# A selective-scan and mixture-of-experts kernel: the first stretch rebuilt, with the first scan unit fed by TensorE instead of by DMA

## The reference, cut to what matters

```python
xn = x * rsqrt(mean(x * x) + eps) * norm_w          # of the layer-normalised x
xi, z = split(xn @ W_in)                            # 256 channels each
xc = silu(causal_conv(xi, conv_w, 4 taps) + conv_b)
dt, Bm, Cm = split(xc @ W_x, [64, 16, 16])
dt = softplus(dt @ W_dt + b_dt)                     # 256 channels
dA = exp(dt[..., None] * A);  dBu = (dt * xc)[..., None] * Bm[:, :, None, :]
h = scan over time of  h = dA * h + dBu             # 256 channels x 16 states
y = (sum over states of h * Cm + D_skip * xc) * silu(z)
s = xn_in + y @ W_out
# experts: softmax over 8 logits, the two largest kept and renormalised;
# out = sum over experts of score_e * (relu(xn @ W1_e + b1_e) @ W2_e + b2_e)
```

## Time and profile before

| | before |
|---|---|
| median of 3 runs | 320.62 us |
| the profiled execution | 321.84 us |
| its span, first to last instruction | 320.0 us |
| busy: PE, DVE, ACT, POOL | 274.6, 275.3, 223.5, 234.6 us |
| DVE's first product and first scan | start at 38.15 and 39.61 us |
| DVE's last instruction | starts at 316.62 us |

### The profile page before, as it was taken

One profiled execution on the slowest core, in us unless ns is written; L12 is line 12 of the kernel. 1 busy time (PEld: TensorE's weight loads), 2 busy tenths in 40 slices (PEclk: granted clock), 3 DMA queues, 4 the chain that ended last, 5 costly groups with the idle time before them and its releaser, 6 DMA issues. The chain is left out here.

```text
span 320.0 us, 4220 instructions
## 1 busy us (share of the span) xinstructions
PE 274.6 (86%) x1223; PEld 140.9 (44%) x1223; DVE 275.3 (86%) x324; ACT 223.5 (70%) x434; POOL 234.6 (73%) x223
## 2 busy tenths in 40 slices
PE   0682699969899999697999999878999998899983
PEld 0331334434644653134566464126554564462472
DVE  3697299975999989997999989899999999999973
ACT  1157288599858896779758975999675684787620
POOL 2207055458899996666989998849989897889764
PEclk9996959999999999789799999999999999999997
DMA  6929990005182830041743800050289600000002
GB/s 170 306 70 210 246 199 3 0 0 123 39 182 61 197 66 0 0 117 20 161 101 68 199 0 3 0 124 11 59 181 203 152 0 0 2 1 1 0 3 66
DMA packets 16758, 26.76 MB, mean 84 GB/s; under 512 B 4264, under 2 KB 9759, under 8 KB 16735
## 3 DMA queue, kind: packets, MB, share of 16 engines
q1 hardware_dynamic: 16246, 25.44, 34.1%
q10 hardware_dynamic: 488, 1.05, 1.1%
HBM read 8.52 MB, written 1.18 MB: 30 GB/s over the span
## 5 line engine op out<-in xcount | busy, mean ns | idle before, releaser
L376 POOL TENSOR_TENSOR hc<-hs,Ct 128x512 f32<-128x512 f32 x126 | 157.7, 1275 | 34.4 <-DVE hs L807 32.7
L807 DVE TENSOR_TENSOR_SCAN hs<-dec,pdbu 128x1024 f32<-128x1024 f32 x64 | 146.3, 2285 | 8.2 <-ACT dec L507 2.6
L507 ACT ACTIVATE dec<-rep,negA 128x512 f32<-128x512 f32 x128 | 87.6, 722 | 8.7 <-DMA rep<-dt_u 5.7
L798 DVE TENSOR_TENSOR pdbu<-rep,pB 128x1024 f32<-128x1024 f32 x64 | 78.6, 1228 | 11.9 <-DMA rep<-dt_u 6.5
L980 PE MATMUL px<-xnT,w 128*128 128x512 f32 x128 | 65.4, 619 | 7.9 <-ACT xnT L566 5.9
L986 PEld LDWEIGHTS px<-w,hT 128*128 128x128 f32 x512 | 62.0, 196 | 18.7 <-ACT hT L622 9.7
L986 PE MATMUL px<-w,hT 128*128 128x128 f32 x512 | 64.6, 282 | 4.7 <-ACT hT L622 4.7
L622 ACT ACTIVATE hT<-px,cols 128x512 f32<-128x512 f32 x64 | 43.2, 690 | 29.6 <-PE px L980 15.6
L461 POOL TENSOR_TENSOR acc<-acc,ysc 128x512 f32<-128x512 f32 x29 | 37.4, 1290 | 14.1 <-ACT ysc L611 9.5
L611 ACT ACTIVATE ysc<-px,score 128x128 f32<-128x128 f32 x116 | 32.8, 366 | 16.5 <-PE px L986 16.5
L909 PE MATMUL py<-hc,rsel 128*32 128x512 f32 x256 | 41.7, 610 | 1.8 <-POOL hc L376 1.8
(11 more groups left out here) (111 smaller groups left out, 235.9 us busy)
## 6 DMA issues: line engine op xcount, KB each, us to landing
rep<-dt_u SPq DMA_DIRECT2D x124, 128.0 KB, 2.4
Ct<-c_rows SPq DMA_DIRECT2D x16, 256.0 KB, 5.0
w<-in_L_ffn_W SPq DMA_DIRECT2D x1, 1024.0 KB
out<-xn SPq DMA_DIRECT2D x4, 256.0 KB, 2.5
x_sb<-in_L_attn_x SPq DMA_DIRECT2D x1, 768.0 KB, 5.2
hc<-in_L_attn_conv_w ACTq DMA_DIRECT2D x1, 512.0 KB, 4.4
rep<-dt_u ACTq DMA_DIRECT2D x4, 128.0 KB, 3.9
x_sb<-in_L_attn_x SPq DMA_DIRECT2D x1, 256.0 KB, 5.2
```

Source lines behind the costliest of these rows:

```text
L376: eng.tensor_tensor(hc[:, n % HC_RING, i, :], hs[:, n % HS_RING, i, :], Ct[:, k % 2, j, :], ALU.mult).then_inc(hc_last if n == UNITS - 1 e ...
L507: act.activation(dec[:, n % DEC_RING, i, :], rep[:, q, 0, :], ACT.Exp, scale=negA[:, q, j:j + 1])\
L798: dve.tensor_tensor(pdbu[:, :, :], rep[:, 2 * pair:2 * pair + 2, 1, :], pB[:, m % 2:m % 2 + 1, :].to_broadcast([P, 2, CH]), ALU.mult).then ...
L807: dve.tensor_tensor_scan(hs[:, n % HS_RING].rearrange("p b t -> p (b t)"), dec[:, n % DEC_RING].rearrange("p b t -> p (b t)"), pdbu[:, :, ...
```

## The change

x of chunk 0 comes in two halves, issued by SP and by ACT, and each is normalised, transposed and copied on its own. The taps come as one row, which TensorE spreads to `pdbu`; DVE weighs them in eight pieces of 128. Selector matrices are built by POOL instead of DVE. `keep_busy` adds small TensorE matmuls whose result nobody reads. For the first unit TensorE spreads `xc` and the parts of `dt` with selectors `csel` (jobs `x0`, `x1`, `d0`, `d1`): `dec` comes from `d0` and `d1` directly, and `u * B` is built as `dt * (xc * B)`, with `xc * B` formed by POOL. The replicas of the first four blocks are then wanted from unit 1 on, and SP issues blocks 2 and 0, POOL blocks 3 and 1 (ACT none). POOL does the roots of chunks 1 to 3 (`rest_roots`) behind these issues. The C product is one instruction of 1024. The slot numbers of `EARLY`, `TABLE`, `STEPS` and `START` are all new.

```diff
-NORM = [range(0, TPC), range(TPC, TILES)]
+NORM = [range(0, TPC // 2), range(TPC // 2, TPC), range(TPC, TILES)]
-PRE_JOBS = ["tr", "xc0", "xc1", "dt", "v0", "v1", "tn", "m0a"]
+PRE_JOBS = ["tr", "xc0", "xc1", "dt", "x0", "v0", "x1", "v1", "d0", "d1", "tn", "m0a"]
...
-    "silu": [12], "log1p": [13, 16], "correct": [17, 20], "sum_dt": [16, 18], "times_dt": [20, 28],
+    "silu": [11], "log1p": [13, 17], "correct": [18, 20], "sum_dt": [18, 18], "times_dt": [23, 29],
...
-    "gate": [0, 1, 3, 5, 6], "gate_e": [0], "gate_p": [2, 3, 4],
+    "second": [0], "gate": [2, 3, 4, 4, 7], "gate_e": [0], "gate_p": [1, 3, 5],
...
+BUSY = {"row": 8, "rows": 4, "tr": 2, "xc1": 2}
...
+        def replicas(eng, q, soft=False):
+            b, r = divmod(q * GD, P)
+            for i in range(GROUP):
+                eng.dma_start(rep[GD * i:GD * (i + 1), q], dt_u[r:r + GD, b])\
+                    .then_inc(rep_soft[q // 2] if soft else rep_in[q // 2], 16)
...
-            sp.dma_start(x_sb[:, 0], xv_dram[:, 0:TPC, :]).then_inc(x_first, 16)
+            sp.dma_start(x_sb[:, 0, 0:TPC // 2], xv_dram[:, 0:TPC // 2, :]).then_inc(x_in[0], 16)
+            sp.dma_start(win[:, :], W_in[:, :]).then_inc(w_in, 16)
...
                 for q in (2 * pair, 2 * pair + 1):
-                    if k == 0 and q == 1:
-                        continue
...
+                    if k > 0 or q >= 2 * HALF_PAIRS or q % 2 == 0:
+                        replicas(sp, q)
...
-            for i in range(2):
-                eng.tensor_tensor(hc[:, n % HC_RING, i, :], hs[:, n % HS_RING, i, :], Ct[:, k % 2, j, :],
-                                  ALU.mult).then_inc(hc_last if n == UNITS - 1 else hc_done, 1)
+            eng.tensor_tensor(hc[:, n % HC_RING], hs[:, n % HS_RING], Ct[:, k % 2, j:j + 1, :].to_broadcast([P, 2, CH]),
+                              ALU.mult).then_inc(hc_last if n == UNITS - 1 else hc_done, 1)
...
-            inverse_roots(0)
-            inverse_roots(1)
+            first_roots()
+            selectors()
+            pool.wait_ge(B_copied, 1)
+            for i in range(2):
+                wait_emptied(pool, f"x{i}", 0)
+                pool.tensor_tensor(xB[:, i], xB[:, i], B_first, ALU.mult).then_inc(xB_done, 1)
+            pool.wait_ge(far_done, 1)
+            for q in (3, 1):
+                replicas(pool, q, True)
+            rest_roots()
...
-            act.dma_start(cwb.rearrange("p d k -> p (d k)"),
-                          conv_w.rearrange("d a k -> a (d k)").to_broadcast([P, DIN * TAPS])).then_inc(w_tap, 16)
+            act.dma_start(x_sb[:, 0, TPC // 2:TPC], xv_dram[:, TPC // 2:TPC, :]).then_inc(x_in[1], 16)
+            act.dma_start(cw_row.rearrange("p a b -> p (a b)"), conv_w.rearrange("d a k -> a (d k)")).then_inc(w_row, 16)
...
+                elif job in ("d0", "d1"):
+                    i = int(job[1])
+                    act.wait_ge(negated, GROUP)
+                    ins = act.activation(dec[:, 0, i, :].rearrange("p (b t) -> p b t", b=BPC)[:, :, 1:],
+                                         src[:, :].rearrange("p (b t) -> p b t", b=BPC)[:, :, 1:], ACT.Exp,
+                                         scale=negA[:, i, 0:1])
...
+                if n == 0:
+                    for i in range(2):
+                        wait_emptied(dve, f"d{i}", 0)
+                        dve.wait_ge(xB_done, i + 1)
+                        dve.tensor_tensor(pdbu[:, i, :], bank_of(f"d{i}", 0)[:, :], xB[:, i, :], ALU.mult)\
+                            .then_inc(dbu_done if i else dbu_half, 1)
+                    return
...
+            def keep_busy(count):
+                for _ in range(count):
+                    pe.matmul(pB[:, 1, 0:P], ident[:, :], ident[:, :], start=True, stop=True)
+            keep_busy(BUSY["row"])
+            pe.wait_ge(w_row, 16)
+            for h in range(2):
+                last = pe.matmul(pdbu[:, h, :], ones_row[:, :], cw_row[:, h, :], start=True, stop=True)
+            last.then_inc(cw_spread, 1)
+            keep_busy(BUSY["rows"])
             pe.wait_ge(w_rows, 16 * N_ROWS)
...
+                elif job == "d0":
+                    other = px[(j + 1) % AUX]
+                    pe.wait_ge(l_done, 1)
+                    pe.matmul(dst[:, :], copies(0), lg1p[:, 0, :], start=True, stop=False)
+                    wait_emptied(pe, *JOBS[j + 1 - AUX])
+                    pe.matmul(other[:, :], copies(1), lg1p[:, 0, :], start=True, stop=False)
+                    pe.wait_ge(lsum_done, 1)
+                    last = pe.matmul(dst[:, :], copies(0), corr[:, 0, :], start=False, stop=True)
...
```

More of the change, by code:

```diff
@@ L241, in mamba_moe @@
         c_out, c_in = sem("c_out"), [sem(f"c_in{i}") for i in range(2)]
-        rep_in = [sem(f"rep_in{i}") for i in range(PAIRS)]
+        rep_in, rep_soft = [sem(f"rep_in{i}") for i in range(PAIRS)], [sem(f"rep_soft{i}") for i in range(HALF_PAIRS)]
         e_done, l_done = sem("e_done"), sem("l_done")
@@ L303, in wait_added, with first_quad, wait_replicas, decays @@
                 eng.wait_ge(acc_added, pool_experts.index((k, e)) + 1)
+        def first_quad(k, pair):
+            return 1 if (k, pair) == (0, 0) else 0
+        def wait_replicas(eng, k, pair):
+            early = pair < HALF_PAIRS
+            eng.wait_ge(rep_in[pair], N_REP * (k + 1) - (N_REP // 2 if early else 0))
+            if k == 0 and early:
+                eng.wait_ge(rep_soft[pair], N_REP // 2)
+        def decays(n):
+            return 2 * (n - 1)
+        def replicas(eng, q, soft=False):
[3 more added lines that the diff above has]
+                    .then_inc(rep_soft[q // 2] if soft else rep_in[q // 2], 16)
         block = ctx.enter_context(nc.Block())
@@ L359, in _ @@
                 for pair in range(PAIRS):
-                    repeat_dt_u(k, pair)
+                    repeat_dt_u(k, pair ^ 1 if k == 0 and pair < HALF_PAIRS else pair)
             for k in range(CHUNKS):
@@ L402, in _, with first_roots @@
             pool.memset(one[:, :], 1.0).then_inc(ones, 1)
-            def inverse_roots(g):
+            pool.memset(ones_row[:, :], 1.0).then_inc(row_set, 1)
+            pool.memset(dec[:, 0, :, 0:CH:SEQ], 0.0).then_inc(zeroed, 1)
+            def first_roots():
+                for g in range(2):
+                    t = slice(NORM[g].start, NORM[g].stop)
+                    pool.wait_ge(ln_mv, g + 1)
+                    pool.tensor_scalar(me[:, t], mv[:, t, 1], 1.0 + EPS, EPS * EPS, ALU.mult, ALU.add).then_inc(rms_me, 1)
+                    pool.wait_ge(rms_me, g + 1)
+                    pool.wait_ge(consts, 3)
+                    pool.tensor_tensor(rr[:, t], me[:, t], mhalf[:, t], ALU.pow).then_inc(rms_r, 1)
+                pool.tensor_scalar(ve[:, 0:TPC], mv[:, 0:TPC, 1], 1.0, EPS, ALU.mult, ALU.add).then_inc(ln_ve, 1)
+                pool.wait_ge(ln_ve, 1)
+                pool.tensor_tensor(rstd[:, 0:TPC], ve[:, 0:TPC], mhalf[:, 0:TPC], ALU.pow).then_inc(ln_rstd, 1)
+                pool.tensor_scalar(me[:, 0:TPC], mv[:, 0:TPC, 0], -1.0, None, ALU.mult).then_inc(rms_me, 1)
+                pool.wait_ge(rms_me, 3)
+                pool.wait_ge(ln_rstd, 1)
+                pool.tensor_tensor(off_n[:, 0:TPC], me[:, 0:TPC], rstd[:, 0:TPC], ALU.mult).then_inc(off_done, 1)
@@ L501, in decay @@
                 k, j, pair = place(n)
-                if j == 0 and i == 0:
-                    act.wait_ge(rep_in[pair], N_REP * (k + 1))
+                if j == first_quad(k, pair) and i == 0:
+                    wait_replicas(act, k, pair)
                 if n >= DEC_RING:
@@ L537, in normalise @@
             def normalise(k):
-                act.wait_ge(off_done, 2)
+                act.wait_ge(off_done, 3 if k else 1)
                 for i in range(TPC):
@@ L857, in _ @@
                     scan(n // 2) if n % 2 else times_B(n // 2)
+                if n == START["second"][0]:
+                    correction(0, 1)
+                    softplus_sum(dve, 0, 1)
+                    times_dt(0, 1)
                 if n == 2 * UNITS - 1:
@@ L924, in fill @@
                         last = pe.transpose(dst[:, i * P:(i + 1) * P], xn[:, k, i, :], ident[:, :])
+                elif (job, k) == ("tr", 0):
+                    for g in range(2):
+                        pe.wait_ge((rows_half, rms_xr)[g], 1)
+                        for i in NORM[g]:
+                            last = pe.transpose((dst, py[:, 0])[g][:, i * P:(i + 1) * P], xr[:, i, :], ident[:, :])
+                        if g == 0:
+                            last.then_inc(tr_half, 1)
                 elif job == "tr":
```

262 lines of the change are left out of this document (161 added, 101 removed), and 29 rows, old and new, of the table TABLE.

## The result

The changed kernel takes 308.99 us, the median of 4 runs (308.73 to 311.73), against 320.21 (318.68 to 320.76) for the kernel before. The ratio of the means is 0.9676 with a 95% interval of 0.9611 to 0.9741. By the medians that is 11.2 us less, by the means 10.4; 6.2 were forecast.

The account below looks back on a forecast made before the run. DVE's scan and `pdbu` bound the time behind the first unit, a chain the time ahead, then POOL's queue. Span 320.0 - 5.5 (front) + 1.0 (wide product) - 1.0 (slots) - 0.7 (tail) = 313.8, timed 314.4 us; range 309 to 320.5.

Parts of the forecast that it names:

- front and first unit: Start of the kernel: convolution at 11.0, `far_done` at 24.05, first scan without replicas at 30.3 instead of 39.61 us.
- Replicas no longer bind. But POOL does.: Second and third units: pair 1 lands near 30.5, pair 0 near 35; POOL's queue then holds DVE's third scan.
- POOL's issue, taken as 1.0 us: POOL's queue behind `far_done`: eight DMA issues take 8.0 us, delaying roots, C product and `gp`; fourth scan 5.5 us earlier.
- The rival of cheap issues: POOL's queue: issues cost 0.59 us each, 8.7 us gained at the front, 311.2 us in all; chance 0.2.
- the factor of 1.8: POOL's issue price: POOL about 1.8 times dearer than DVE on products of 512, applied to SP's 0.59 us, gives 1.06.
- The upper bound, 2.05 us: POOL's issue price at most: an issue into a full queue; front 2.9 us lost, 322.8 us in all; slower rival's chance 0.1.
- the new slots, booked at 1.0 us gained: Steady stretch: chunk 1's correction one slot later gives more cover for DVE's 3.1 us wait; 3 lost to 4 gained.
- the gain is swallowed: Rival: ACT sets the pace between 60 and 80 us, so DVE's gained time turns into waits, 320.3 us; chance 0.1.
- the wide product, booked at 1.0 us lost: POOL's C product as one instruction of 1024: DVE steps with two SBUF inputs wait longer on shared ports; 0 to 4 lost.
- The tail, booked at 0.7: End of the kernel: two experts instead of three stand at TensorE's end, 0.7 us gained (0 to 1.5).
- the 3.3 us at the convolution: Front: convolution starts at 11.0 instead of 14.28 us, 3.3 us gained (2 to 4.5).
- the likeliest case's own range: Whole kernel: the forecast case, 311.5 to 318 us, chance 0.6.

Follow-up runs that it names:

- the reissue alone: Kernel before, with block 1's four replica DMAs issued by SP right behind block 0's instead of by ACT: 320.66 us, 0.9981.
- the wait put back: Changed kernel, with its first scan also waiting for pair 0's replicas, which it doesn't use: 315.92 us, 0.9856.

## Why the prediction was right, and where it wasn't

The direction and the mechanism of the front held. The range held by the ratio (0.9676 of 320.62 is 310.2 us), with the median at its low end, 308.99 against 309. The terms for POOL's issues, for the slots with the wide product, and for the tail were mis-sized, all of them too pessimistic.

**Right: front and first unit.** `far_done` at 25.03 (24.05 forecast), convolution at 11.45 (11.0), |v| at 19.20 (18.8), first scan at 30.48 (30.3), second product at 32.90 (32.65). `far_done` was 1.0 us late: 0.45 of it at the convolution, most of the rest in one step, the sum `dt_u<-zr,xv`, which took 1.34 us instead of 0.69 while POOL was at its two products for `xB` (21.12 to 23.63). The first scan doesn't hang on `far_done`, so it came as forecast. That a unit fed by TensorE starts without DMA, and that this is where the gain lies, is shown from both sides: the reissue alone gave 0.9981, and the wait put back cost 6.5 us at the first scan.

**Half right: "Replicas no longer bind. But POOL does."** For DVE's products of units 1 and 2 no wait for a replica is left. But pairs 1 and 0 landed at 32.67 and 36.43, not near 30.5 and 35, and pair 0 held the third unit by way of ACT (0.67 us), while POOL's `gp` was there 0.65 us before MAX wanted it.

**Mis-sized: POOL's issue, taken as 1.0 us, is 0.52.** The term "8.0 us of issues" was 4.13, and the gain at the fourth scan 8.1 us instead of 5.5. The rival of cheap issues, 0.59 each and 8.7 us, had this right with a chance of 0.2. The wrong turn was the factor of 1.8: POOL's and DVE's time for arithmetic on 512 elements says nothing about POOL's time to hand over a DMA. The nearest row of the same kind of work, SP's 0.59 us, was the better guide. The page figure beside it (the Trainium skill, "DMA: Bandwidth & Descriptors", "Latency and other measured facts") is a time to the first byte; it is not the engine's time per issue, and the row of 4.13 us for eight shows that the 8 us it was set beside don't follow from it. Nor do SP's 591 ns agree with the page's 600: they are how long the issuing instruction lasts, and no row here shows a first byte. The upper bound, 2.05 us for an issue "into a full queue", is a duration only; that a full queue made it so, no row shows. The queue's mechanism itself was right: with sixteen issues of 0.50 us MAX waited for `gp`.

**Mis-sized: the new slots, booked at 1.0 us gained.** With the kernel before they give 0.7%, about 2 us, which lay within the booked range. (The 11 us of waits behind that range are 14.0 by its own rows, 5.8 and 8.2.) But on the new front they decide: without them 0.9930, with them 0.9676 and 0.9703, 7 to 8 us. The prediction judged the slots on the old front and then added the two as if they were independent. Its rival "the gain is swallowed" at ACT between 60 and 80 us describes what happens with the slots of before, only that it begins at TensorE and ahead of 60: DVE waits 2.8 and 3.2 us for ACT's decays, and the wait for 1 + exp is back at 3.1. So the swallowing was real, and the slots are what averts it; the sentence that ACT's burst "moves with DVE" was wrong as a reason.

**Not settled: the wide product, booked at 1.0 us lost.** By itself it gave 1.0018, with 1.0 us lost inside the interval; on the new front it was rather a gain, within the noise. The mechanism was right and larger than booked, 2.6 us on the 16 steps of the kernel before, with the longest wait twice as long as before (1.95 us over the usual 0.69, before 1.05); the interval allows at most 1.7 us lost, so something gave part of it back. POOL's products took 149.3 us there instead of 157.7; whether it was that, no run shows. In the changed kernel, by duration:

```profile
L853 DVE SCALAR_TENSOR_TENSOR xv<-xv,ev x7: 665/895/1947, 27.4 to 212.2; 128x512 f32<-128x512 f32 x7
L860 DVE TENSOR_TENSOR dt_u<-dt_u,xc x8: 683/693/1585, 24.2 to 226.0; 128x512 f32<-128x512 f32 x8
```

The first's median is 0.90 us (before 0.69) and its longest 1.95 (1.65); the second's are 0.69 and 1.59 (0.69 and 1.74). The rule of the Trainium skill ("SBUF — State Buffer", "Who interferes with whom") fits the outliers. With the narrow product on the new front the 15 steps take 12.5 us, with the wide one 13.8.

**The tail, booked at 0.7,** gave 1.7 us. The last experts on DVE start 3.46 us after the last scan's start, without a wait; in the earlier trace rows it was 5.15 us with one of 1.54:

```profile
298.00 2.33 DVE L925 SCALAR_TENSOR_TENSOR acc<-px,score,acc 128x128 f32<-128x128 f32 x8
```

**Credited to the wrong edits.** The prediction let x's halves bring `xr` forward as one of the reasons for the 3.3 us at the convolution. Waiting for the whole of x changes nothing (0.9677), as long as its two halves are loaded at once. And the unread matmuls, costed at "at most 0.5 us", keep the tap row from TensorE for 1.95 us (3.78 to 5.73); without them the kernel is 2.8 us faster by medians. The landing assumed for the tap row, 5.96, was late by over 2 us, and that the first product of the row started near it, at 5.73, was a coincidence.

**The sum.** Forecast of the span: 5.5 front, net 0 between, 0.7 tail, 6.2 us. Measured: 8.1, 3.1, 1.7. The terms' errors all point the same way, 2.6 + 3.1 + 1.0. By medians it is 1.6 us less than the profiles show, since the profiled execution of the kernel before lay that far above its median. So the time came to the low end of the range, and the likeliest case's own range, from 311.5, missed it by the median and by the ratio.

## What to carry to other kernels

An earlier front is worth only as much as the hand-written order behind it lets through: measure the two parts alone and together, since here 0.7% and 0.7% made 3.2%. Price an unseen issue by the nearest row of the same kind of work, not by an engine's speed at arithmetic. And when an engine is given filler work ahead of a DMA's landing, look when the data really came: filler holds the engine against it.
